# Turning 36 of 96 expert weight pieces in the steps of the first attention stage

## The chip, the cores and the metric

The kernel runs on one core of a Trainium2 chip. The time is device microseconds of one execution, the median of several. Engines are named as the profile names them: PE (TensorE), PEld (its weight loads), DVE (VectorE), ACT (ScalarE), POOL (GpSimd), SP (the queue that starts most DMAs).

## The reference

Two decoder layers on 16 sequences of 64 tokens with 128 features (1024 tokens), each a chain of three blocks, each block followed by the residual sum and a layernorm:

```python
x = ln(x + L0_attn(x))            # 16 heads of 8, rope, causal
x = ln(x + L0_xattn(x, ctx))      # 16 heads of 8, padding mask
x = ln(x + L0_ffn(x))             # 8 experts, inner 512, best 2 of 8 for each token
x = ln(x + L1_attn(x))            # 16 heads of 64
x = ln(x + L1_xattn(x, ctx))
x = ln(x + L1_ffn(x))             # ternary weights, gelu, layernorm inside
```

The third block is what the weights of the change belong to:

```python
for e in range(8):
    hidden = silu(x @ wg[e].T) * (x @ wu[e].T)     # wg, wu: 512 x 128
    out += combine[e] * (hidden @ wd[e].T)         # wd: 128 x 512
```

The matrix unit needs all three of them transposed. One expert has 3 matrices of 4 square pieces of 128x128, so 8 experts have 96 pieces. All is float32.

## The kernel before

The 1024 tokens are 8 tiles of 128. The two first blocks (`a0`, self attention with rope, and `a1`, cross attention; class `Narrow`) are one stream `pre` of 16 tiles. `stream_pe`, `stream_act`, `stream_dve` and `stream_pool` each walk through 18 steps j = 0 to 17. In step j, PE does in this order: the scores of tile j-2 (`s_pe`, L540 to L551), the transpose of the attention output of tile j-5 (`y_pe`, L583), q and k of tile j (`qk_pe`, L512), v of tile j-2 (`v_pe`, L524), the transposes of the probabilities of tile j-3 (`t_pe`, L430), the output projection of tile j-5 (`o_pe`, L587), the weighing of v of tile j-4 (`va_pe`, L567), and the transpose of a finished tile (`x_pe`, L372). ACT does in step j: `y_act` (L633), `qk_act` (L601 or L610), `v_act` (L621), `pt_act` (L439), `exp_act` (L420), `x_act` (L377). DVE does `y_dve` (L677, L681), `max_dve` (L404, L414), `r_dve` (L389, L325, L327), `qk_dve` (L642 to L654, or L667). POOL does the blocks of k (L691), rope's cosine product (L703) and the square root and normalization of the layernorm. Each engine works strictly in its own order, and semaphores join them.

k of a tile lands in columns 0 to 127 of PSUM bank 6 (`B_K`) and q in the same columns of bank 7 (`B_Q`). Columns 128 to 511 of both are unused in these steps.

The expert weights lie in `WALL`, [128, 8 experts, 3 matrices, 512]. SP starts their loads: experts 0 to 3 directly after the masks, experts 4 to 7 after the wide attention's weights. All 24 loads raise one semaphore, `s_raw`.

After the stream comes a written-out part, the drain (`drain_pe`, `drain_act`, `drain_dve`, `drain_pool`), in which the last tiles of `a1` end, the router's logits are made, the two best experts of each token chosen (`choose`), the row of each token in the sorted list found (`place`), and the tokens scattered to DRAM by POOL's indirect DMAs (`scatter`, L1438). Between these steps of PE and ACT stand 24 groups of weights: `weights_pe` turns one matrix (4 pieces) in one of banks 0 to 3, `weights_copy` copies the 512 columns back in place. Groups 0 to 9 are strewn between the drain's steps, 10 to 12 stand before the last `rank_pe`, 13 to 23 behind it.

Then the routed block runs (`moe.pe` and its partners): 23 blocks of 128 sorted rows, each loaded from DRAM (`XG`), turned (L1522), multiplied with the gate (L1550), up (L1558) and down (L1581) weights. Its first instruction on PE waits for the last copy of weights and for the first block's load, which SP starts once all 16 scatters have landed.

Of the kernel before, what the change touches and what calls it, by code (L numbers as in the profile page):

```python
# [15 lines left out]
P = 128  # L16
# [5 lines left out]
PAIRS = HEADS // 2  # L22
EXPERTS, INNER = 8, 512
CH = INNER // P
BANK = 512
LN_EPS = 1e-5

# [51 lines left out]
def decoder_kernel(nc, A, out):  # L79
    with ExitStack() as ctx:  # L80
# [142 lines left out]
        s_b = [sem("first_biases_loaded"), sem("second_biases_loaded")]  # L223
        s_m = sem("masks_loaded")
        s_raw = sem("expert_weights_loaded")
        s_wide = sem("wide_weights_loaded")
        s_out_w = sem("wide_output_weights_loaded")
        s_sep = sem("wide_weights_separated")
# [949 lines left out]
        def stream_pe(pe, tiles, extra, last):  # L1178
            for j in range(last):
                a = at(tiles, j - 2)  # L1180
                if a:
                    a.stage.s_pe(pe, a)
                y = at(tiles, j - 5)
                if y:
                    y.stage.y_pe(pe, y)
                b = at(tiles, j - 1)
                if b:
                    b.stage.qkw_pe(pe, b)
                b = at(tiles, j)
                after_v = a and a.stage.wide  # L1190
                if b and not after_v:
                    b.stage.qk_pe(pe, b)
                if a:
                    a.stage.v_pe(pe, a)
                extra(pe, j, False)
                t, v = at(tiles, j - 3), at(tiles, j - 4)
                if v and v.stage.wide:
                    v.stage.va_pe(pe, v)
                if t:
                    t.stage.t_pe(pe, t)  # L1200
                if v:
                    v.stage.ty_pe(pe, v)
                first_v = v and not v.stage.wide and y and y.stage.wide
                if first_v:
                    v.stage.va_pe(pe, v)
                if y:
                    y.stage.o_pe(pe, y)
                if v and not first_v and not v.stage.wide:
                    v.stage.va_pe(pe, v)
                if v:  # L1210
                    v.stage.vb_pe(pe, v)
                if b and after_v:
                    b.stage.qk_pe(pe, b)
                for x in turned(tiles, j):
                    x.stage.x_pe(pe, x)
                extra(pe, j, True)
# [96 lines left out]
        class Routed:  # L1313
# [3 lines left out]
            def __init__(self, prev):  # L1317
                self.prev = prev
                self.w_mm, self.w_cp = Mark("expert_weights_transposed"), Mark("expert_weights_copied")
                self.g_mm, self.lg = Mark("logits_made"), Mark("logits_copied")  # L1320
                self.top, self.topi, self.topf = Mark("logits_sorted"), Mark("experts_ranked"), Mark("ranked_experts_cast")
                self.oh, self.sel, self.bef = Mark("choices_made"), Mark("choices_joined"), Mark("choices_counted")
                self.r_mm, self.rk, self.pm, self.posf, self.pos = (
                    Mark("ranks_made"), Mark("ranks_based"), Mark("ranks_chosen"), Mark("rows_summed"), Mark("rows_made"))
                self.map = Mark("blocks_mapped")
                self.diff, self.e2, self.den = Mark("logit_difference_made"), Mark("second_exponential_made"), Mark("pair_sum_made")
                self.p1, self.p2 = Mark("first_weight_made"), Mark("second_weight_made")
                self.xt_mm, self.xgt = Mark("block_transposed"), Mark("block_copied")
                self.gate_mm, self.u_mm, self.silu, self.mul = (
                    Mark("gates_projected"), Mark("ups_projected"), Mark("silu_made"), Mark("hidden_made"))  # L1330
                self.d_mm, self.ycp = Mark("downs_projected"), Mark("expert_output_copied")
                self.we_act, self.we_pool = Mark("first_blocks_weights_brought"), Mark("blocks_weights_brought")
                self.acc = Mark("expert_added")
                self.norm = Norm("experts")


            def weights_pe(self, pe, g):
                e, w = g // 3, g % 3
                if g == 0:
                    pe.wait_ge(s_raw, 48 * EXPERTS)  # L1340
                if g >= 4:
                    pe.wait_ge(*self.w_cp.at(g - 3))
                elif g >= 2:
                    pe.wait_ge(*pre[-1].pt_read(g - 2))
                else:
                    pe.wait_ge(*pre[-1].s_read())
                for c in range(CH):
                    m = pe.transpose(PS[:, g % 4, P * c:P * (c + 1)], WALL[:, e, w, P * c:P * (c + 1)], ident)
                m.then_inc(self.w_mm.sem, 1)

            def weights_copy(self, act, g):
                act.wait_ge(*self.w_mm.at(g + 1))
                act.activation(WALL[:, g // 3, g % 3, :], PS[:, g % 4, :], ACT.Copy).then_inc(self.w_cp.sem, 1)


            def logits_pe(self, pe, k):
# [171 lines left out]
                act.activation(XGT[:, j % 3, :], PS[:, 6, 0:P], ACT.Copy).then_inc(self.xgt.sem, 1)  # L1528

            def bring_act(self, act, j, e):  # L1530
                act.wait_ge(*self.w_cp.at(3 * EXPERTS))
                act.activation(WE[:, j % 3].rearrange("p w i -> p (w i)"),
                               WALL[:, e, 0:2, :].rearrange("p w i -> p (w i)"), ACT.Copy).then_inc(self.we_act.sem, 1)

# [57 lines left out]
            def pe(self, pe):  # L1592
                last = pre[-1]
                pe.wait_ge(*last.y_read())
                pe.wait_ge(*self.rk.at(len(GROUPS)))
                pe.wait_ge(*self.map.at(8))
                _, e = nc.values_load_multi_w_load_instructions(
                    bi[0:1, 0, 0:BLOCKS], engines=[mybir.EngineType.PE], min_val=0, max_val=EXPERTS - 1,
                    skip_runtime_bounds_check_because="a sum of seven comparisons, each 0 or 1")
                pe.wait_ge(*self.w_cp.at(3 * EXPERTS))  # L1600
                self.block_pe(pe, 0)
                self.block_pe(pe, 1)
                for n in range(BLOCKS + 1):
                    if n + 2 < BLOCKS:
                        self.block_pe(pe, n + 2)
                    if n == 8:
                        fc.totals(pe, self.mul.at(n - 1))
                    if n < BLOCKS:
                        self.gate_pe(pe, n)
                    if n == 9:  # L1610
                        pe.wait_ge(*fc.thr.at(2))
                    if n < BLOCKS:
                        self.up_pe(pe, n)
                    if n >= 1:
                        self.down_pe(pe, n - 1, e[n - 1])
                pe.wait_ge(s_sep, 3)
                pe.wait_ge(*self.silu.at(BLOCKS))
                wide.weights_pe(pe)
                pe.wait_ge(*self.xgt.at(BLOCKS))
                fct.pe(pe, [0])  # L1620
                pe.wait_ge(*self.ycp.at(BLOCKS))
                fct.pe(pe, [1])
                pe.wait_ge(*self.mul.at(BLOCKS))
                wide.products_pe(pe)
                fc.project_bias(pe)
                fc.means_pe(pe)
                pe.wait_ge(*fc.bias.at(1))
                self.turn_pe(pe, (0,))
# [50 lines left out]
            def pool(self, pool):  # L1679
# [1 line left out]
                _, e = nc.values_load_multi_w_load_instructions(  # L1681
                    bi[0:1, 0, 0:BLOCKS], engines=[mybir.EngineType.Pool], min_val=0, max_val=EXPERTS - 1,
                    skip_runtime_bounds_check_because="a sum of seven comparisons, each 0 or 1")
                pool.wait_ge(*self.w_cp.at(3 * EXPERTS))
                for j in range(2, BLOCKS):
                    self.bring_pool(pool, j, e[j])
                    if j in (6, 9, 12):
# [91 lines left out]
                (moe.rank_pe if late else moe.logits_pe)(pe, 0)  # L1779

        def pre_act(act, j, late):
            if j == 1 and late:
                later.copies(act, 0)
            if j in (2, 3) and late:
                weights.copies(act, 0, [j - 2])
            if j == len(pre) and not late:
                moe.logits_act(act, 0)
# [38 lines left out]
        def drain_pe(pe):  # L1826
# [25 lines left out]
            moe.logits_pe(pe, 3)  # L1852
            weights_pe(pe, 10, 13)
            moe.rank_pe(pe, 3)
            weights_pe(pe, 13, 3 * EXPERTS)

        def drain_act(act):
            moe.logits_act(act, 1)
# [14 lines left out]
            moe.x_act(act, 7)  # L1873
            weights_act(act, 9, 10)
            moe.logits_act(act, 3)
            weights_act(act, 10, 3 * EXPERTS)
            act.activation(warm[:, 0:1], half[:, :], ACT.Silu)

        def drain_dve(dve):
# [64 lines left out]
        def _(sp):  # L1944
# [19 lines left out]
                    load(mri[half + 2 * j:half + 2 * j + 2, :, :], mask[:, 0], s_m)  # L1964

            def load_expert(e):
                for w, name in enumerate(("L0_ffn_wg", "L0_ffn_wu")):
                    load(WALL[:, e, w].rearrange("p (c h) -> p c h", c=CH),
                         A[name][e].rearrange("(c i) h -> i c h", c=CH), s_raw)
                load(WALL[:, e, 2], A["L0_ffn_wd"][e], s_raw)  # L1970

            for e in range(4):
                load_expert(e)
# [102 lines left out]
```

## Time and profile before

| | us |
|---|---|
| median of 3 runs | 368.32 (366.67 to 368.34) |
| the profiled execution, whole | 367.42 |
| its span, first to last instruction | 365.6 |

Times in the profile run from the start of the span. The profiled execution has 1.8 us around its span. PE is busy for 90% of the span. The engines' rows in the timeline end with the idle time ahead of the group, in brackets, and what ended it.

### The profile page before, as it was taken

How to read it: one execution, taken by the hardware profiler on the slowest of the kernel's cores; microseconds unless marked ns; L12 is line 12 of the kernel's file. 1: busy time of each engine (PE TensorE's matmuls, PEld its weight loads, DVE VectorE, ACT ScalarE, POOL GpSimd, SP SyncE). 2: the span in 40 equal slices, each digit the busy share in tenths (PEclk: the TensorE clock that was granted, in tenths of full speed). 3: DMA queues.
4: the chain of work that ended last, by engine and by line, in shares of the span. 5: the costliest groups of instructions: out<-in, count | busy, mean ns of one | idle time of the engine just before them, and what ended most of it. 6: DMA issues, size and time to landing. Idle time of an engine off the chain costs nothing.

```text
span 365.6 us, 9896 instructions
## 1 busy us (share of the span) xinstructions
PE 328.4 (90%) x3774; PEld 259.7 (71%) x3774; DVE 236.4 (65%) x561; ACT 182.6 (50%) x383; POOL 203.0 (56%) x289
## 2 busy tenths in 40 slices
PE   3879999998888599999995997899999999999993
PEld 2546767777677499999994864676677676777673
DVE  2698987778865034573337477845666677877685
ACT  2457766777578533233313243453355436667641
POOL 2856998885777155543306755321222257486785
PEclk9989999999999699999998799999999999999998
DMA  6899997000001111111101110000000000000001
GB/s 184 229 310 285 293 336 203 2 2 3 31 29 53 58 31 52 50 46 45 39 22 38 46 31 14 2 2 2 0 4 2 1 2 3 2 2 2 4 22 38
DMA packets 35993, 22.98 MB, mean 63 GB/s; under 512 B 4196, under 2 KB 33900, under 8 KB 35820
## 3 DMA queue, kind: packets, MB, share of 16 engines
q1 hardware_dynamic: 34636, 19.64, 18.5%
q0 software_dynamic: 1024, 2.10, 1.9%
q8 instruction: 31, 0.51, 0.6%
q10 hardware_dynamic: 288, 0.62, 0.5%
q14 instruction: 14, 0.11, 0.1%
HBM read 14.61 MB, written 7.73 MB: 61 GB/s over the span
## 4 chain that ended last, share of the span: by engine, by line
PE 71%; DVE 15%; issue 5%; POOL 3%; ACT 3%; DMA 2%; SPq 1%; POOLq 0%; ACTq 0%; DVEq 0%
PE banks L845 7%; PE banks L430 7%; PE banks L832 7%; PE banks L1550 6%; PE banks L1558 6%; PE banks L1581 6%; PE banks L540 5%; PE banks L567 5%; PE banks L876 3%; PE banks L512 2%; PE banks L524 2%; PE banks L1033 2%; DVE mx L404 2%; PE banks L583 2%; PE banks L859 2%
## 5 line engine op out<-in xcount | busy, mean ns | idle before, releaser
L691 POOL TENSOR_TENSOR KB<-KT,cst 128x512 f32<-128x512 f32 x48 | 49.3, 1048 | 7.8 <-DVE KT L651 5.6
L404 DVE TENSOR_REDUCE mx<-banks 128x16 f32<-128x1024 f32 x32 | 38.6, 1206 | 12.0 <-PE banks L551 10.1
L439 ACT ACTIVATE PT<-banks 128x512 f32<-128x512 f32 x64 | 34.7, 594 | 23.0 <-PE banks L430 21.8
L882 ACT ACTIVATE U<-banks 128x512 f32<-128x512 f32 x40 | 23.9, 597 | 37.6 <-PE banks L845 22.6
L1573 DVE TENSOR_TENSOR PT<-banks,PR 128x512 f32<-128x512 f32 x23 | 15.9, 691 | 41.1 <-PE banks L1558 36.8
L1538 POOL COPY U<-WALL 128x1024 f32 x21 | 21.9, 1043 | 35.7 <-PE banks L1558 35.5
L332 POOL TENSOR_SCALAR ve<-mv 128x1 f32<-128x1 f32 x40 | 9.2, 231 | 50.8 <-DVE mv L327 50.4
L420 ACT ACTIVATE PR<-PR 128x1024 f32<-128x1024 f32 x32 | 33.9, 1058 | 4.0 <-DVE PR L414 3.7
L430 PE MATMUL banks<-cst,PR 128*128 128x128 f32 x256 | 34.8, 279 | 0.5 <-POOL PR L911 0.5
L832 PE MATMUL banks<-XT,WQKV 128*128 128x128 f32 x256 | 32.8, 290 | 0.4 <-ACT XT L1751 0.4
L845 PE MATMUL banks<-WALL,XT 128*64 128x512 f32 x128 | 29.8, 601 | 3.1 <-DVE U L882 2.8
L832 PEld LDWEIGHTS banks<-XT,WQKV 128*128 128x128 f32 x256 | 31.3, 203 | 1.1 <-ACT XT L1751 0.7
L540 PE MATMUL banks<-KB,QS 64*64 64x512 f32 x192 | 27.9, 635 | 3.6 <-DVE PR L414 2.2
L430 PEld LDWEIGHTS banks<-cst,PR 128*128 128x128 f32 x256 | 27.6, 141 | 4.1 <-issue 2.0
L414 DVE TENSOR_TENSOR PR<-banks,mx 128x1024 f32<-128x1024 f32 x24 | 29.4, 1224 | 0.8
L567 PE MATMUL banks<-VB,PT 128*64 128x18 f32 x768 | 26.7, 212 | 0.0
L567 PEld LDWEIGHTS banks<-VB,PT 128*64 128x64 f32 x768 | 24.3, 138 | 3.0 <-issue 0.5
L1550 PE MATMUL banks<-XGT,U 128*128 128x128 f32 x184 | 25.3, 282 | 0.0
L882 DVE COPY U<-banks 128x512 f32<-128x512 f32 x24 | 16.2, 686 | 13.7 <-PE banks L845 10.9
L334 POOL TENSOR_TENSOR rstd<-ve,half 128x1 f32<-128x1 f32 x40 | 23.2, 579 | 3.3
L1707 POOL DMA_INDIRECT KB<-routed_rows,pos x16 | 15.9, 993 | 16.4 <-DMA routed_rows<-YS 12.3
L1581 PE MATMUL banks<-WALL,PT 128*128 x184 | 24.4, 276 | 0.6 <-DVE YS L1589 0.6
(192 smaller groups left out, 700.0 us busy)
## 6 DMA issues: line engine op xcount, KB each, us to landing
routed_rows<-zero SPq DMA_DIRECT2D x1, 4544.0 KB, 19.3
WALL<-in_L_ffn_wg_dram SPq DMA_DIRECT2D x8, 256.0 KB, 5.0
WALL<-in_L_ffn_wu_dram SPq DMA_DIRECT2D x8, 256.0 KB, 5.3
WALL<-in_L_ffn_wd_dram SPq DMA_DIRECT2D x8, 256.0 KB, 5.6
U<-in_L_attn_W_qkv_dram SPq DMA_DIRECT2D x1, 1536.0 KB, 23.0
XG<-routed_rows SPq DMA_DIRECT2D x23, 64.0 KB, 1.8
routed_rows<-YS SPq DMA_DIRECT2D x23, 64.0 KB, 1.6
cst<-shape_constants ACTq DMA_DIRECT2D x1, 537.0 KB, 4.5
```

The costliest lines, as they stand in the source:

```text
L404: dve.tensor_reduce(mx[:, n % 2, :], s, AX.X, ALU.max).then_inc(self.max.sem, 1)
L420: act.activation(p, p, ACT.Exp, scale=self.scale).then_inc(self.exp.sem, 1)
L430: t = pe.transpose(PS[:, B_PT + m, P * (r % 4):P * (r % 4 + 1)], PR[:, n % 2, P * r:P * (r + 1)], ident)
L439: act.activation(PT[:, n % 2, 4 * m:4 * m + 4, :].rearrange("p r q -> p (r q)"), PS[:, B_PT + m, :], ACT.Copy).then_inc(self.pt.sem, 1)
L540: pe.matmul(PS[q, B_S + g, :], QS[f, n % 3, q], KB[f, n % 2, b].rearrange("p h k -> p (h k)"), start=True, stop=False)
L567: m = pe.matmul(PS[64 * b:64 * b + 64, B_Y, w * r:w * (r + 1)], PT[:, n % 2, r, 64 * b:64 * b + 64], VB[:, n % 3, r, b].rearrange("p a e - ...
L691: pool.tensor_tensor(KB[:, n % 2, b], bc(KT[:, n % 2, b, :], 1, 8), bc(cst[:, C_HEAD:C_HEAD + 8], 2, SEQ), ALU.mult).then_inc(self.kb.sem, 1)
L832: m = pe.matmul(PS[:, bank, P * k:P * (k + 1)], WQKV[:, f // 2, P * u:P * (u + 1)], XT[:, P * i:P * (i + 1)], start=True, stop=True)
L845: m = pe.matmul(PS[64 * a:64 * a + 64, bank, :], XT[:, SEQ * (2 * i + b):SEQ * (2 * i + b + 1)], WVO[:, a, 4 * g:4 * g + 4, :].rearrange(" ...
L882: return eng.activation(o, s, ACT.Copy) if part == 0 else eng.tensor_copy(o, s)
L1550: m = pe.matmul(PS[:, j % 2, P * c:P * (c + 1)], WE[:, j % 3, 0, P * c:P * (c + 1)], XGT[:, j % 3, :], start=True, stop=True)
L1581: m = pe.matmul(PS[:, 7, 0:P], HT[:, j % 2, c, :], WALL[:, e, 2, P * c:P * (c + 1)], start=(c == 0), stop=(c == CH - 1))
```

## The change

The pieces of experts 0, 1 and 2 (36 of 96) are turned in steps 3 to 9 of the stream, 3 pieces at a time. Steps 3 to 7 have two groups each, one in columns 128 to 511 of the k bank and one in those of the q bank; steps 8 and 9 have one each, in the q bank. On PE they stand between `s_pe` and `y_pe`; on ACT each group is copied back by one instruction of 384 columns at the end of the step. PE waits, before it writes a bank again, for the copy of the group that was in it; step 10 waits for all 12. The loads of experts 0, 1 and 2 get a semaphore each. The drain has 15 groups of 4 pieces in place of 24; its written-out order is the same up to group 12, and 2 groups, not 11, stand behind the last `rank_pe`.

```diff
@@ stream_pe
                 if a:
                     a.stage.s_pe(pe, a)
+                if tiles is pre:
+                    moe.early_pe(pe, j)
                 y = at(tiles, j - 5)
@@ class Routed
+            def pieces(self, j):
+                if not 3 <= j <= 9:
+                    return []
+                first, banks = (6 * (j - 3), (B_K, B_Q)) if j <= 7 else (30 + 3 * (j - 8), (B_Q,))
+                return [(first // 3 + k, bank) for k, bank in enumerate(banks)]
+
+            def early_pe(self, pe, j):
+                if j == 10:
+                    pe.wait_ge(*self.e_cp.at(4 * EARLY))
+                for g, bank in self.pieces(j):
+                    if g % 4 == 0:
+                        pe.wait_ge(s_raw0[g // 4], 48)
+                    if bank == B_K or j > 7:
+                        for s in pre[j - 1].stage.qk_read(pre[j - 1].i):
+                            pe.wait_ge(*s)
+                    if g >= 2:
+                        pe.wait_ge(*self.e_cp.at(g - 1 if j <= 7 else g))
+                    w = WALL[:, g // 4].rearrange("p w i -> p (w i)")
+                    for n in range(3):
+                        k = 3 * (g % 4) + n
+                        m = pe.transpose(PS[:, bank, P * (n + 1):P * (n + 2)], w[:, P * k:P * (k + 1)], ident)
+                    m.then_inc(self.e_mm.sem, 1)
+
+            def early_act(self, act, j):
+                for g, bank in self.pieces(j):
+                    act.wait_ge(*self.e_mm.at(g + 1))
+                    w = WALL[:, g // 4].rearrange("p w i -> p (w i)")
+                    k = 3 * (g % 4)
+                    act.activation(w[:, P * k:P * (k + 3)], PS[:, bank, P:4 * P], ACT.Copy).then_inc(self.e_cp.sem, 1)
+
             def weights_pe(self, pe, g):
-                e, w = g // 3, g % 3
+                e, w = EARLY + g // 3, g % 3
                 if g == 0:
-                    pe.wait_ge(s_raw, 48 * EXPERTS)
+                    pe.wait_ge(s_raw, 48 * (EXPERTS - EARLY))
@@ pre_act
+            if late:
+                moe.early_act(act, j)
@@ drain_pe (drain_act likewise)
             moe.rank_pe(pe, 3)
-            weights_pe(pe, 13, 3 * EXPERTS)
+            weights_pe(pe, 13, 3 * (EXPERTS - EARLY))
```

## Rows read from the trace of the kernel before

**Rows 1.** The page, busy time of PE: us, share, instructions.
```profile
PE 328.4 (90%) x3774; PEld 259.7 (71%) x3774; DVE 236.4 (65%) x561; ACT 182.6 (50%) x383; POOL 203.0 (56%) x289
```
**Rows 2.** The chain that ended last, steps 9 and 10: start us, us, what.
```profile
51.14 1.02 PE banks L540 x8
52.38 0.26 PE banks L583
...
56.02 1.02 PE banks L540 x8
```
**Rows 3.** The same chain, steps 4 and 5.
```profile
24.57 1.84 PE banks L540 x8
...
26.83 1.15 PE banks L512 x4
...
28.47 1.02 PE banks L430 x8
...
31.77 0.27 PE banks L583
```
**Rows 4.** Timeline of PE, 20 to 128 us: start, us, work, idle before.
```profile
21.79 0.60 PE L271 MATMUL banks<-cst,U 128*128 128x128 f32 x4
24.57 1.84 PE L540 MATMUL banks<-KB,QS 64*64 64x512 f32 x8 [2.18 <-DVE PR L414]
...
36.95 0.33 PE L583 MATMUL banks<-cst,ysb 128*128 128x128 f32 x1 [0.56 <-DVE ysb L681]
...
42.14 0.33 PE L583 MATMUL banks<-cst,ysb 128*128 128x128 f32 x1 [0.24 <-DVE ysb L681]
...
47.43 0.33 PE L583 MATMUL banks<-cst,ysb 128*128 128x128 f32 x1 [0.34 <-DVE ysb L681]
...
112.78 5.00 PE L1348 MATMUL banks<-cst,WALL 128*128 128x128 f32 x44
```
**Rows 5.** Timeline of ACT, steps 6 and 7, and the drain's end.
```profile
41.02 0.28 ACT L377 ACTIVATE XT<-banks 128x128 f32<-128x128 f32 x1
42.50 0.37 ACT L633 ACTIVATE yT<-banks,bvc 128x128 f32<-128x128 f32 x1 [1.20 <-PE banks L583]
...
113.45 5.50 ACT L1353 ACTIVATE WALL<-banks 128x512 f32<-128x512 f32 x11 [0.84 <-PE banks L1348]
```
**Rows 6.** Timeline of DVE, step 6.
```profile
39.40 0.29 DVE L389 TENSOR_TENSOR R<-banks,XR 128x128 f32<-128x128 f32 x1
...
41.79 0.29 DVE L681 TENSOR_TENSOR ysb<-banks,rs 128x128 f32<-128x128 f32 x1
```
**Rows 7.** Timeline of SP's queue: the last load of expert 0.
```profile
15.95 0.50 SPq L1946 DMA_DIRECT2D WALL<-in_L_ffn_wd_dram  x1
```
**Rows 8.** DMA issues, 15.9 to 16.4 us: count, size, us to landing.
```profile
WALL<-in_L_ffn_wd_dram SPq DMA_DIRECT2D x1, 256.0 KB, 3.9
```
**Rows 9.** Windows of 1 us: five engines' busy, granted clock, DMA.
```profile
27.00:28.00 1.00, 1.00 (x6) 0.78 (x8) 1.00 (x1) 0.37 (x1) 0.82 (x1) 0.50 1.21 316
28.00:29.00 1.00, 1.00 (x13) 0.93 (x14) 0.96 (x2) 0.83 (x3) 0.54 (x1) 0.90 1.09 295
...
117.00:118.00 1.00, 0.79 (x8) 0.55 (x5) 0.00 (x0) 1.00 (x3) 0.70 (x1) 1.00 0.19 66
```
**Rows 10.** The chain that ended last, end of drain and first block.
```profile
118.00 2.23 DMA routed_rows<-X,pos
...
120.40 1.75 DMA XG<-routed_rows
...
122.29 0.46 PE banks L1522
...
124.55 1.72 PE banks L1550 x8
```
**Rows 11.** Timeline of POOL, its last scatter.
```profile
118.00 0.96 POOL L1438 DMA_INDIRECT routed_rows<-X,pos  x1 [0.30 <-issue]
```
**Rows 12.** The copies of weights, line L1353: min, median, max ns, first and last start.
```profile
L1353 ACT ACTIVATE WALL<-banks x24: 591/601/703, 101.2 to 118.2; 128x512 f32<-128x512 f32 x24
```

More of the change, by code:

```diff
@@ L24 @@
 CH = INNER // P
+EARLY = 3
 BANK = 512
@@ L225, in decoder_kernel @@
         s_raw = sem("expert_weights_loaded")
+        s_raw0 = [sem("first_expert_weights_loaded_%d" % e) for e in range(EARLY)]
         s_wide = sem("wide_weights_loaded")
@@ L1319, in __init__ @@
                 self.w_mm, self.w_cp = Mark("expert_weights_transposed"), Mark("expert_weights_copied")
+                self.e_mm, self.e_cp = Mark("early_weights_transposed"), Mark("early_weights_copied")
                 self.g_mm, self.lg = Mark("logits_made"), Mark("logits_copied")
@@ L1352, in weights_copy @@
                 act.wait_ge(*self.w_mm.at(g + 1))
-                act.activation(WALL[:, g // 3, g % 3, :], PS[:, g % 4, :], ACT.Copy).then_inc(self.w_cp.sem, 1)
+                act.activation(WALL[:, EARLY + g // 3, g % 3, :], PS[:, g % 4, :], ACT.Copy).then_inc(self.w_cp.sem, 1)
             def logits_pe(self, pe, k):
@@ L1530, in bring_act @@
             def bring_act(self, act, j, e):
-                act.wait_ge(*self.w_cp.at(3 * EXPERTS))
+                act.wait_ge(*self.w_cp.at(3 * (EXPERTS - EARLY)))
                 act.activation(WE[:, j % 3].rearrange("p w i -> p (w i)"),
@@ L1599, in pe @@
                     skip_runtime_bounds_check_because="a sum of seven comparisons, each 0 or 1")
-                pe.wait_ge(*self.w_cp.at(3 * EXPERTS))
+                pe.wait_ge(*self.w_cp.at(3 * (EXPERTS - EARLY)))
                 self.block_pe(pe, 0)
@@ L1683, in pool @@
                     skip_runtime_bounds_check_because="a sum of seven comparisons, each 0 or 1")
-                pool.wait_ge(*self.w_cp.at(3 * EXPERTS))
+                pool.wait_ge(*self.w_cp.at(3 * (EXPERTS - EARLY)))
                 for j in range(2, BLOCKS):
@@ L1875, in drain_act @@
             moe.logits_act(act, 3)
-            weights_act(act, 10, 3 * EXPERTS)
+            weights_act(act, 10, 3 * (EXPERTS - EARLY))
             act.activation(warm[:, 0:1], half[:, :], ACT.Silu)
@@ L1966, in load_expert @@
             def load_expert(e):
+                s = s_raw0[e] if e < EARLY else s_raw
                 for w, name in enumerate(("L0_ffn_wg", "L0_ffn_wu")):
                     load(WALL[:, e, w].rearrange("p (c h) -> p c h", c=CH),
-                         A[name][e].rearrange("(c i) h -> i c h", c=CH), s_raw)
-                load(WALL[:, e, 2], A["L0_ffn_wd"][e], s_raw)
+                         A[name][e].rearrange("(c i) h -> i c h", c=CH), s)
+                load(WALL[:, e, 2], A["L0_ffn_wd"][e], s)
             for e in range(4):
```

## The prediction

> **What bounds the kernel now.** I read the page first: PE is busy for 90% of the span [rows 1]. That share is an average, so the two stretches that the change touches, the stream's steps 3 to 10 and the drain's end, were read in the chain of waits and in each engine's timeline.
>
> In the steady stream PE is the bound. Step 9's scores start at 51.14 and step 10's at 56.02, a period of 4.88 us, and the chain is made of PE alone; scores to the next transpose of y (`y_pe`) take 1.24 us [rows 2]. Whatever is put on PE there is paid in full. In steps 6 to 8 PE stands still for 0.56, 0.24 and 0.34 us ahead of `y_pe`, each time for DVE's `ysb` [rows 4]; this is just where the early groups go. DVE itself waits there for PE's output projection: from its sum R at 39.40 to the end of `ysb` at 42.08 it takes 2.7 us, and then PE goes on [rows 6]. So these steps are a loop through both engines, and PE's room in it is no more than its idle time. In step 3 there is more: PE has done its last work there by 22.4 and waits 2.18 us for DVE's subtraction before step 4 begins at 24.57 [rows 4].
>
> At the drain's end, the last 11 groups take PE from 112.78 to 117.8 and ACT to 118.95 [rows 4, 5]. The first block does not wait for them. Its transpose starts at 122.29, after the tile's load (120.40, 1.75 us), which itself follows POOL's last scatter (issued 118.00, landed 120.23) [rows 10, 11]. Between the last copy and that transpose lie 3.3 us.
>
> **What goes: nine groups at the end of the drain.** Groups 0 to 12 keep their places, so the drain's own chain stays. Of the 11 groups behind the last `rank_pe` two remain: PE ends some 4 us and ACT 9 x 0.5 = 4.5 us earlier [rows 5]. What is late next is what was late before, the scatters on POOL, which wait for no weights. ACT's work between its last copy and the first block moves forward with the copy and was finished in time anyway. I count the gain as 0.
>
> **What comes: 36 transposes on PE.** 44 of them took 5.0 us at the full clock, so 0.113 apiece, 0.34 for a group of three, 0.67 for a step with two groups [rows 4, 9]. No row has a copy of 384 columns. 128 columns took 0.28 us and 512 took 0.60 [rows 5, 12]; these two are its bounds, and the value on the line between them is 0.49, which I take. The copies of a step are 0.98 us on ACT. Behind them in ACT's queue stands the next step's `y_act`, ahead of which ACT idles 1.20 us [rows 5], waiting for `y_pe`, which now comes later still; so they delay no other work of ACT. What they can delay is PE: the second group of a step waits for the second copy of the step before, and `y_pe`, q, k, v and the probabilities' transposes are queued behind it.
>
> Step by step, as the lateness of `y_pe` (or of the scores) against the trace of before:
>
> Step 3: the early groups come up at 19.8 us. The last load of expert 0 is issued at 15.95 and lands 3.9 us later, at 19.85 [rows 7, 8], just in time. The 0.67 us goes into the 2.18 us of idle time that follows. DVE's work there is queued behind its own subtractions and does not notice. Cost 0; without that cover it would be 0.67.
>
> Step 4: here the granted clock is at its lower level, 1.2 GHz, having fallen in the idle time before: 0.50 until 28 us, 0.90 in the next one [rows 9]. In this stretch the scores take 1.84 us against 1.02 [rows 2, 3]. The six transposes stand at 26.83, 0.67 x 2 = 1.34 us at half clock. They use up the slow time, so q, k and v after them run at the full clock: about 0.83 us in place of the 1.64 between 26.83 and 28.47 [rows 3]. Net +0.53.
>
> Step 5: +0.67, and about 0.10 of waiting: ACT's exponential follows PE's transposes, and its two copies end 0.4 us after the scores, while PE's first group fills only 0.34. `y_pe`, at 31.77 before [rows 3], comes 1.30 late.
>
> Step 6: two groups, but 0.56 us of idle time [rows 4] take most of it, since the loop through DVE brings `ysb` at its own pace. +0.25, total 1.55.
>
> Step 7: idle time 0.24, and with the small gap before it 0.31. ACT's `x_act` ended at 41.30 [rows 5], 4.35 us after `y_pe` at 36.95; two copies and a semaphore make 5.4, and one group 0.34 more: `y_pe` 5.74 us after the last one, where it was 5.19 [rows 4]. +0.55, total 2.10.
>
> Step 8: one group, which waits for both copies of step 7: +0.13, total 2.23. Step 9: one group in a step bound by PE, less a rest of idle time: +0.27, total 2.50. Step 10 waits for one copy that is 0.3 us early. From there every step is bound by PE and the lateness is carried to the end.
>
> Sum: 2.5 us on the profiled execution's 367.42 us (365.6 of span, 1.8 around it): 369.9. That execution lies 0.9 under the median of the three runs; the middle of all four executions is 367.9. I add the 2.5 to that: 370.4.
>
> Bounds: at the lower end the copies never hold PE (-0.4) and the clock does not fall before step 4 (-1.0, below): +1.1. At the upper end none of steps 4 to 9 has room: 30 transposes x 0.113 = 3.4, with the copy waits (0.5) and a whole extra 0.67 at half clock: +4.6.
>
> A rule of the Trainium skill speaks against the change more strongly. During 44 transposes in a row the granted clock stayed at 1.00 and each took 0.113 us [rows 4, 9]. The page "TensorE: Matmul & The Clock Gate", Part 4 (PE-mode transpose), says that the full clock is not engaged by transposes. By that rule the early groups would run at 0.225 us apiece, 36 x 0.113 = 4 us more than here, and the sum would be up to 6.5. The trace doesn't agree with it, and I give it no share.
>
> **The rivals.**
>
> A, the clock stays up in step 4. With the early groups in step 3, PE's idle time ahead of 24.57 shrinks from 2.18 to about 1.5 us. For it: less idle time than the gap that the clock fell in. Against it: 1.5 us is still a gap, and the work before it is the same. If so, the scores of step 4 take 1.24 instead of 2.26 with their masks, and `y_pe` of step 5 comes about 1.0 earlier: +1.5, 368.9 on the profiled execution, 369.4 on the middle. Half of that would be within what can be told.
>
> B, ACT becomes the loop. Copies of 0.60 rather than 0.49 and a longer way from copy to PE (0.15 more) add 2 x 0.11 + 0.15 = 0.37 to each of the steps 5 to 8, 1.5 us in all: +4.0, 371.9. For it: ACT's last copy of step 6 ends, by my sum, at almost the moment at which PE's first group does. Against it: 512 columns took 0.60, and 384 should take less.
>
> C, faster: the last copies do hold the first block. If the first block's transpose followed the last copy and not the load, the end of the drain would come up to 4.5 us earlier, and with the 2.5 paid in the stream the time would be 2.0 less: 365.9. It decides only if ACT's last copy, or what follows it, ends after the tile's load. For it: the block's first instruction does wait for that copy. Against it: 3.3 us lie between them, and POOL's last scatter is issued 0.95 us before the last copy ends, and lands 1.3 after [rows 5, 10, 11].
>
> D, the weights come too late. If expert 0 lands some 4 us after the early groups come up, q and k of tile 3 and the first transposes of probabilities wait behind them, 2.2 us of which the idle time doesn't take: +4.7, 372.6. For it: at 19.85 against 19.8 there is no margin. Against it: up to 1.5 us of lateness is covered.
>
> **How the numbers follow.** Forecast 0.50 (369.0 to 371.6), A 0.23, B 0.11, C 0.09, D 0.07. Predicted 370.4. The range 368.5 to 372.4 takes in the forecast, A's middle, B and the lower half of D, and leaves out C and the tails. What a measurement of this kernel can tell from no change is about 0.5%, 1.8 us. Forecast is over that in eight cases of ten (0.40), A in a third (0.08), B and D always (0.18): 0.66, of which I take off 0.06 for the chance in the runs: slower 0.60. C and a little of A: faster 0.09. The rest, 0.31, is the same.
>
> **What would show it.** Period of the scores in steps 5 to 8: about 5.6, 5.5 and 5.4 us in place of 5.2, and 4.88 again from step 10. The first block's transpose at about 124.8, as far behind POOL's last scatter as before, with PE idle ahead of it for some 8 us in place of 4.5. ACT's early copies at 0.49. The granted clock near 25 us separates A. A period above 6 us in step 6 or 7, with PE waiting for ACT, would be B; a first block's transpose at under 122 us would be C; PE idle near 20 us for the load, D. I am wrong if the scores of step 12 stand less than 1 us later than before, or if the stretch from the last scatter to the first block has shrunk.

## The result: 0.4% slower, and the clock decides over as much as the change

| | before | after |
|---|---|---|
| median us (20 runs each) | 367.65 (366.28 to 371.79) | 368.72 (367.56 to 370.24) |
| profiled execution, whole / span | 367.42 / 365.6 | 370.17 / 368.4 |

The ratio is 1.0041 with a 95% interval of 1.0028 to 1.0055: 1.5 us (1.0 to 2.0); the two medians lie 1.1 apart. The forecast was +2.5 us (370.4); its range of 368.5 to 372.4 holds the measured 368.7 at its lower edge, and the size is the +1.5 of rival A. Part of that agreement is luck, as the comparison of single profiles below shows.

The profile after. Here is the page's line of busy time; beside [rows 1], the work on PE is the same.

```profile
PE 328.7 (89%) x3774; PEld 260.7 (71%) x3774; DVE 236.3 (64%) x561; ACT 182.9 (50%) x386; POOL 202.8 (55%) x289
```

The timeline of PE after, steps 3 to 9, where [rows 4] had its idle times (scores L542, early groups L1363, `y_pe` L585):

```profile
20.77 0.87 PE L1363 MATMUL banks<-cst,WALL 128*128 128x128 f32 x6 [0.63 <-DMA WALL<-in_L_ffn_wd_dram]
...
24.79 1.09 PE L542 MATMUL banks<-KB,QS 64*64 64x512 f32 x8 [0.86 <-issue]
25.67 0.43 PE L550 MATMUL banks<-caus,idb 64*64 64x512 bf16 x4
26.30 0.84 PE L1363 MATMUL banks<-cst,WALL 128*128 128x128 f32 x6 [0.21 <-ACT WALL L1371]
...
29.97 1.09 PE L542 MATMUL banks<-KB,QS 64*64 64x512 f32 x8
...
31.92 0.27 PE L585 MATMUL banks<-cst,ysb 128*128 128x128 f32 x1
...
37.19 0.27 PE L585 MATMUL banks<-cst,ysb 128*128 128x128 f32 x1
...
42.72 0.27 PE L585 MATMUL banks<-cst,ysb 128*128 128x128 f32 x1
...
47.96 0.27 PE L585 MATMUL banks<-cst,ysb 128*128 128x128 f32 x1
...
56.73 1.09 PE L542 MATMUL banks<-KB,QS 64*64 64x512 f32 x8
```

The idle times ahead of `y_pe` are gone, so is most of that ahead of step 4, and step 4's scores take 1.09 us where they took 1.84: the clock did not fall there. PE is now the bound from step 5 on: `y_pe` comes every 5.27, 5.53 and 5.24 us. In windows around step 4, before, then after (the number behind the five engines is the granted clock):

```profile
24.00:28.00 4.00, 3.44 (x18) 1.53 (x20) 3.57 (x8) 1.42 (x2) 3.13 (x4) 0.60 1.14 317
```
```profile
24.00:28.00 4.00, 3.00 (x31) 1.92 (x32) 3.90 (x9) 2.61 (x6) 3.31 (x5) 1.00 1.13 316
```

By step 10 the scores stand at 56.73 against 55.95, only 0.78 us later, and 0.23 of that was there at step 3. At step 12 it is 0.79 (66.48 against 65.69). The profiled execution is 2.8 us longer in all, and lost most of the rest, 1.8 us, at two places where nothing was added. One is the drain's start (1.2 us up to the first block), where the clock fell at 92.8, after PE's 1.07 us of idle time at 90.7, an idle time that the kernel before has too. Windows of 1 us, after; then PE's timeline there, whose row before took 1.09 us for the same transposes:

```profile
92.00:93.00 1.00, 1.00 (x12) 0.34 (x12) 0.90 (x6) 0.28 (x1) 0.66 (x2) 0.91 0.00 0
93.00:94.00 1.00, 1.00 (x9) 0.18 (x1) 0.67 (x3) 0.00 (x0) 0.89 (x2) 0.50 0.00 0
```
```profile
91.73 0.30 PE L374 MATMUL banks<-cst,X 128*128 128x128 f32 x1 [1.07 <-issue]
...
94.65 1.84 PE L432 MATMUL banks<-cst,PR 128*128 128x128 f32 x8
```

The other is the first block, which begins at 124.28, 4.42 us behind POOL's last scatter where it was 4.29 [rows 10, 11]: the relief brought nothing. PE had been idle for 8.56 us, not 4.51, and the clock rose 6.1 us after the first transpose, not 4.9. From that transpose to the first product with `wd` (called the cold start below) it took 7.67 us (before: 7.10).

```profile
124.28 0.45 PE L1558 MATMUL banks<-cst,XG 128*128 128x128 f32 x1 [8.56 <-DMA XG<-routed_rows]
...
126.34 1.93 PE L1586 MATMUL banks<-XGT,U 128*128 128x128 f32 x8
128.06 1.92 PE L1594 MATMUL banks<-XGT,U 128*128 128x128 f32 x8
...
131.95 1.06 PE L1617 MATMUL banks<-WALL,PT 128*128 x8
```

So one profile of each does not give the price of the change: it has other falls of the clock in it. The executions of all comparisons but the 20 of the kernel before in the table have their mean granted clock on record, and the spans come in lots by it. Of 111 executions of the kernel before, 42 have a mean of 0.977 or 0.978 and a median span of 364.6 us, 57 have 0.973 and 366.1, and 12 lie between 366.7 and 371.1. Of 34 after, 19 have 0.973 and 366.4, 13 have 0.969 or 0.964 and 368.1, and two have 370.2 and 371.1. Lot against lot the change costs 1.8 and 2.0 us, if the lots are paired from the best down. More executions are in the better lot after (19 of 34 against 42 of 111), which gives part of it back. (After, the mean is lower at equal losses, since the clock is down for longer around PE's idle time ahead of the first block: 10.2 us in the profile with doubled copies below, whose mean is 0.973, against 6.8 in the second profile before, at 0.978.) The mean tells how long the clock was down and not where, so that this pairing is argued, not shown.

### The profile page after: what moved, and what is told of

It is laid out like the page before. It is cut to its first block, busy times and chain, and to the rows that moved or that the text cites. A ratio compares the mean times of both kernels' runs of the same rounds, so it can differ in the third digit from the quotient of the medians.

```text
span 368.4 us, 9909 instructions
## 1 busy us (share of the span) xinstructions
PE 328.7 (89%) x3774; PEld 260.7 (71%) x3774; DVE 236.3 (64%) x561; ACT 182.9 (50%) x386; POOL 202.8 (55%) x289
## 4 chain that ended last, share of the span: by engine, by line
PE 75%; DVE 11%; issue 5%; POOL 3%; ACT 2%; DMA 2%; SPq 1%; POOLq 0%; DVEq 0%; ACTq 0%
PE banks L432 8%; PE banks L847 7%; PE banks L834 7%; PE banks L569 6%; PE banks L1586 6%; PE banks L542 6%; PE banks L1594 6%; PE banks L1617 6%; PE banks L878 3%; PE banks L514 2%; PE banks L526 2%; PE banks L1035 2%; PE banks L861 2%; PE banks L374 1%; PE banks L1091 1%
## 5 line engine op out<-in xcount | busy, mean ns | idle before, releaser
L1609 DVE TENSOR_TENSOR PT<-banks,PR 128x512 f32<-128x512 f32 x23 | 15.9, 691 | 41.8 <-PE banks L1594 37.5
L432 PE MATMUL banks<-cst,PR 128*128 128x128 f32 x256 | 35.6, 283 | 0.5 <-POOL PR L913 0.5
L542 PE MATMUL banks<-KB,QS 64*64 64x512 f32 x192 | 27.2, 617 | 2.5 <-issue 2.5
L1586 PE MATMUL banks<-XGT,U 128*128 128x128 f32 x184 | 25.4, 283 | 0.0
L1594 PE MATMUL banks<-XGT,U 128*128 128x128 f32 x184 | 25.2, 281 | 0.0
```

Of the source, the lines that this page charges most:

```text
L432: t = pe.transpose(PS[:, B_PT + m, P * (r % 4):P * (r % 4 + 1)], PR[:, n % 2, P * r:P * (r + 1)], ident)
L542: pe.matmul(PS[q, B_S + g, :], QS[f, n % 3, q], KB[f, n % 2, b].rearrange("p h k -> p (h k)"), start=True, stop=False)
L1586: m = pe.matmul(PS[:, j % 2, P * c:P * (c + 1)], WE[:, j % 3, 0, P * c:P * (c + 1)], XGT[:, j % 3, :], start=True, stop=True)
L1594: m = pe.matmul(PS[:, 2 + j % 2, P * c:P * (c + 1)], WE[:, j % 3, 1, P * c:P * (c + 1)], XGT[:, j % 3, :], start=True, stop=True)
```

## The experiments

All are compared with the kernel before on the same chip. "Shift" is the start of the scores of a step, counted from those of step 3 of the same profile; before it is 37.35 us for step 10, after 37.90.

**The kernel before and after once more.** No edit.

> The kernel before once more, for a second profile. Theory: two lots, near 364.6 us of span at a mean clock of 0.977 and near 365.8 at 0.973; a profile of the first shows no fall ahead of step 4 and scores of step 10 some 0.9 us earlier than 55.95. If the lots come from anything else than the clock, the scores stand where they stood.

Median 367.71, ratio 1.0006 (0.9984 to 1.0028). This profile is one of the better lot (0.978, span 365.0). PE's idle time of 2.18 us ahead of step 4 is the same, yet the clock stayed up:

```profile
24.67 1.09 PE L540 MATMUL banks<-KB,QS 64*64 64x512 f32 x8 [2.18 <-DVE PR L414]
...
29.26 1.09 PE L540 MATMUL banks<-KB,QS 64*64 64x512 f32 x8 [0.19 <-DVE PR L414]
```

Step 5's scores come 4.59 us after step 4's, where the first profile had 5.90, and step 10 stands at a shift of 36.37, 0.98 less. The same kernel with the same idle time does the one or the other. The 3.4 us at half clock in step 4 also make up the 0.005 between the two profiles' means (0.973 and 0.978). The 0.98 us are two thirds of the 1.5 between the lots, and for the other 0.5 there is no row.

> The changed kernel once more, for a second profile. Theory (price of the moved groups 1.5 us against a kernel before whose clock stays up in step 4, and the rest is the clock): step 4 at the upper level again, and executions in two lots, near 366.1 us of span without a fall of the clock in the drain and near 368.1 with one. If the fall at 93 us of the first profile belongs to the change, it is in nearly all executions.

Median 368.95, ratio 1.0041 (1.0023 to 1.0060), as at first. The theory held for the lots (8 of 14 near 366.5, 4 near 368.2) but not for this profile, which shows a third thing, span 371.1:

```profile
21.80 1.54 PE L1363 MATMUL banks<-cst,WALL 128*128 128x128 f32 x6 [1.51 <-DMA WALL<-in_L_ffn_wd_dram]
23.14 1.06 PE L514 MATMUL banks<-XT,WT 128*128 128x128 f32 x4
24.13 0.70 PE L526 MATMUL banks<-WT,XT 128*64 128x64 f32 x8
24.75 1.97 PE L432 MATMUL banks<-cst,PR 128*128 128x128 f32 x8
26.52 1.06 PE L273 MATMUL banks<-cst,U 128*128 128x128 f32 x4
27.51 1.09 PE L542 MATMUL banks<-KB,QS 64*64 64x512 f32 x8
```

SP issued expert 0's last load 0.54 us later than in the first profile before, and it took 5.3 us to land instead of 3.9. PE waited 1.51 us from 20.3 on, the clock fell at 20.7, and the rest of step 3 ran at half of it: step 4's scores begin at 27.51, 8.52 us after step 3's, where all other profiles have 5.96 or 5.97: 2.6 us late. So rival D is real, by another way than it was priced: a wait of 1.5 us was to be covered, and what was not covered is the work at half clock. Of 34 executions after, two have spans over 370, this one among them. The clock also fell once in this profile's drain, at 106.0.

**The stream alone.** The early copies go to a spare tile; the drain keeps its 24 groups.

```diff
-   act.activation(w[:, P * k:P * (k + 3)], PS[:, bank, P:4 * P], ACT.Copy)
+   act.activation(SCRATCH[:, g % 6, :], PS[:, bank, P:4 * P], ACT.Copy)
```

> The 12 early groups as in the changed kernel, but copied to a spare tile, and the drain with all its 24 groups: the price of the stream alone. My theory (the drain's relief is worth nothing, the whole difference is PE time in the stream): the same as the changed kernel, 1.0 to 1.9 us above before, near 368.8. Rival (the relief gives back part of a larger price): clearly slower than the changed kernel, 2.5 us or more above before.

Median 369.14, ratio 1.0057 (1.0033 to 1.0081): the change's price without its relief. The shift of step 10 is 37.91, as after, and the last scatter to first block takes 4.37 us. The two ratios lie 0.6 us apart and both are uncertain, so a relief of up to 1.6 us isn't excluded by them; 2.5 us or more is. The lots say less: 366.7 (7 executions at 0.977 and 0.978) and 368.2 (4 at 0.973 and 0.974), 2.1 us over the kernel before in both, where the change had 1.8 and 2.0.

**The relief alone.** `weights_pe(pe, 13, 15)` and its copies in place of groups 13 to 23, nothing early.

> Before, with the last nine groups of the drain left out and nothing added (those weights stay unturned, so that the result is another; the routing is decided ahead of them and stays): the relief alone. My theory: within 0.4 us of before, and the first block's transpose stands as far behind POOL's last scatter as before, with PE idle for 8 us. Rival (the last copies hold the first block): 2 to 4.5 us faster. A second rival (the longer idle time costs clock): 0.5 to 1.5 us slower, with the granted clock at its lower level for longer after the first block.

Median 368.11, ratio 1.0047 (1.0011 to 1.0083). No gain, and by the ratio not the 0 that I expected either. The first block is 4.41 us behind the last scatter, with PE idle for 8.56. The clock went down at 117.9 instead of 120.4 and rose at 128.1 instead of 127.2, and the first block took 7.50 us to its first product instead of 7.10. The ratio lies elsewhere: nine of its 12 executions correspond to the kernel before's lot of 366.1 (they have 365.8), three to the one near 370, and none to that of 364.6. So within a lot the relief changed 0.3 us or less. Why the best lot is missing stays open: it turns on step 4, which this kernel has unchanged and where its profile lost the clock. On this chip 9 of 35 executions before are in that lot, so that 12 in a row outside it would come by chance some three times in a hundred. It was not run again.

**Step 3 alone.** The two early groups of step 3, to the spare tile, whole drain.

> Before, with the two early groups of step 3 alone (copied to a spare tile, the drain whole). Theory of the clock (they shorten PE's idle time ahead of step 4, the clock stays at its upper level there): 0.4 to 0.9 us faster than before, with step 4 at the full clock in the profile. Rival (only the work counts, and it hides in the idle time): the same within 0.2, and the clock falls as in before. If even this cover fails: 0.7 slower.

Median 368.09, ratio 0.9986 (0.9944 to 1.0029): the time does not tell. The profile does: step 4 runs at the upper clock, with 0.82 us of idle time ahead of it:

```profile
24.62 1.09 PE L543 MATMUL banks<-KB,QS 64*64 64x512 f32 x8 [0.82 <-issue]
```

The shift of step 10 is 36.43 against 37.35 and, with the clock up, 36.37. The six transposes cost 0.06 us. This profile, too, has the clock down at the drain's start, from 90.5 to 93.9. It lies in the lot at 0.973 without a fall in step 4. The best lot (5 of 12, at 0.978) has 365.2, which is 0.6 over the kernel before's, not 0.06.

**No group in step 3.** Two groups in each of steps 4 to 7, one in each of 8 to 11. Of the edit this is the main line; the groups are numbered to match, and step 12 waits for all of them.

```diff
-                if not 3 <= j <= 9:
+                if not 4 <= j <= 11:
```

> The changed kernel with its 12 groups in steps 4 to 11 (two a step to 7, then one), none in step 3. Theory: the cover of step 3 is gone, so 6 more transposes are paid (0.7 us), and the clock falls ahead of step 4 again in most executions (0.5 to 0.9): 1.2 to 1.6 us above the changed kernel, 370.0 to 370.4. Rival (what counts is only the number of transposes on PE, wherever they stand): the same as the changed kernel.

Median 371.94, ratio 1.0132 (1.0094 to 1.0170): 4.9 us over before, 3.4 over the change, more than expected. Step 4's scores again have 2.18 us of idle time ahead of them, the clock is at 0.50 from 26 to 29 us, and the six transposes there took 1.54 us:

```profile
24.75 1.09 PE L542 MATMUL banks<-KB,QS 64*64 64x512 f32 x8 [2.18 <-DVE PR L416]
25.98 1.54 PE L1363 MATMUL banks<-cst,WALL 128*128 128x128 f32 x6
...
31.18 1.09 PE L542 MATMUL banks<-KB,QS 64*64 64x512 f32 x8
```

At step 12 the shift is 1.91 us more than after and 2.47 more than before. Both sides have the clock down in step 4 in the second comparison, and in the first only this kernel has. All five executions on record lie at mean clocks of 0.964 to 0.969; the profiled one also lost the clock at the drain's start, which makes up about 1 us of the rest.

**Groups in steps where PE is the bound.** One group of three in each of steps 9 to 15, spare tile, whole drain.

> Before, with seven groups of three transposes in steps 9 to 15, one a step, in the q bank (copied to a spare tile, the drain whole). In these steps PE is the bound and nothing idles. Theory (a group costs its 0.34 to 0.36 us in such a step, and its copy on ACT nothing): 2.4 to 2.5 us above before in executions with the same granted clock, steps of 5.23 us in place of 4.87. Rival (PE reads weights for the next work early and swallows part of it): under 1.5 us.

Median 369.99 of seven executions, ratio 1.0085 (1.0054 to 1.0116), 3.1 us. The lot at 0.978 (four of them) has 367.65 against 364.6, +3.0. The profile is of the slowest execution, with the clock down in step 4 and from 103.7 on besides, but at 1.00 in steps 9 to 16. There the steps are 5.20 us long:

```profile
51.12 1.09 PE L543 MATMUL banks<-KB,QS 64*64 64x512 f32 x8
52.35 0.55 PE L1361 MATMUL banks<-cst,WALL 128*128 128x128 f32 x3
52.74 0.27 PE L586 MATMUL banks<-cst,ysb 128*128 128x128 f32 x1
...
56.32 1.09 PE L543 MATMUL banks<-KB,QS 64*64 64x512 f32 x8
```

A group costs 0.33 us, seven 2.3, and nothing of it is swallowed. The other 0.7 is not in the stream; I have no row for it. The stream alone and step 3 alone have such a surplus too, as said in the next section.

**The copies twice.**

```diff
+                    act.activation(SCRATCH[:, g % 6, :], PS[:, bank, P:4 * P], ACT.Copy)
                     act.activation(w[:, P * k:P * (k + 3)], PS[:, bank, P:4 * P], ACT.Copy)
```

> The changed kernel with every early copy of ACT done twice (first to a spare tile): some 0.8 us more on ACT in each of steps 3 to 7, 0.4 in 8 and 9. The prediction said that the copies already hold PE by 0.1 to 0.2 us a step; by that, each step from 5 to 8 would grow by most of 0.8 and the time by 2.5 to 3 us over the changed kernel. What the profile after says (the second copy ends some 0.3 us before PE's second group asks for it): 0.3 to 0.5 a step, 1.5 to 2 us in all. If ACT has room: nothing.

Median 371.96 of six executions, ratio 1.0159 (1.0106 to 1.0212), 3.2 us over the change's median, and 3.5 in the lot at 0.973 (369.9 against 366.4); the shift of step 10 is 3.20 more (41.10). PE now waits for ACT's copies in each of steps 4 to 8, for example in step 8:

```profile
48.97 1.09 PE L543 MATMUL banks<-KB,QS 64*64 64x512 f32 x8
...
51.04 0.52 PE L1364 MATMUL banks<-cst,WALL 128*128 128x128 f32 x3 [0.77 <-ACT WALL L1375]
```

Steps 4 to 8 are 0.4 to 0.8 us longer, for 0.74 us more of copies (0.37 each). So the copies of the change stand 0 to 0.3 us short of holding PE: ACT's margin is small, yet my copy waits were not there.

**Fills on the changed kernel.** Transposes of the identity into a free bank, read by nobody, 64 of them between the drain and the first block.

```diff
             drain_pe(pe)
+            for _ in range(64):
+                pe.transpose(PS[:, B_Y, 0:P], ident, ident)
```

> The changed kernel with 64 transposes of the identity put on PE in its idle time ahead of the first block (7.2 us of some 8.5), which nobody reads. If the cold start of the first block costs what its rows show (gate, up and gate again 1.7, 1.7 and 1.0 us against 0.9 each), it ends 1.3 to 1.9 us under the changed kernel, near 367.0, and no slower than before. If the first block is bound by its waits and not by the clock: 368.7, and if the filling stands in the way: more.

Median 369.53, ratio 1.0039 (1.0000 to 1.0077): no gain. The clock was still up as the first block began at 123.44, but between the lone transposes of blocks 0 to 2 PE idles 0.46 us twice, after 1.96 us of idle time that the fill had left. The clock fell at 124.5, and gate and up took 1.93 and 1.53 us.

**Fills on the kernel before, in the gaps too.** 12 at the end of step 3, 8 in step 16, 38 behind the drain, and 3 behind each of the first two block transposes.

```diff
                 self.block_pe(pe, 0)
+                filler(pe, 3, B_Y)
                 self.block_pe(pe, 1)
+                filler(pe, 3, B_Y)
```

> Before, with nothing moved, but transposes of the identity that nobody reads in PE's idle times: 12 at the end of step 3, 8 in step 16 ahead of the last transposes of x, 38 behind the drain and 3 each between the first blocks. Theory of the clock (what the changed kernel won in step 4 and lost in the drain is the clock alone): step 4, the drain and the first block run at the upper level, 0.9 and 1.3 to 1.6 us off, 365.0 to 365.8 in the median, and the fills delay nothing. Rival (the fills stand in the way or the clock falls all the same): 367.6 or more.

Median 365.77 (363.99 to 368.20), ratio 0.9972 (0.9945 to 1.0000). Of all kernels here it has the lowest median; the gain over the kernel before is at the edge of the interval, that over the changed one is clear of it. The clock does fall once, in the drain at 101.3. Step 4, the drain's start and the first block are at the upper clock, and the fills delay nothing:

```profile
118.08 4.31 PE L1180 MATMUL banks<-cst 128*128 128x128 f32 x38
122.86 0.30 PE L1532 MATMUL banks<-cst,XG 128*128 128x128 f32 x1 [0.47 <-DMA XG<-routed_rows]
...
124.53 1.11 PE L1560 MATMUL banks<-XGT,U 128*128 128x128 f32 x8
125.47 1.06 PE L1568 MATMUL banks<-XGT,U 128*128 128x128 f32 x8
```

From the first transpose to the first product with `wd` it takes 5.40 us, here and in the two filled kernels that follow, against 6.89 to 8.03 in the profiles without fills at this place: the cold start had cost 1.7 before.

**The same fills on the changed kernel** (8, 72 and twice 3; step 3 has its own groups).

> The changed kernel with unread transposes of the identity in PE's idle times: 8 in step 16, 72 behind the drain, 3 each between the first blocks. Theory: the drain and the first block at the upper level; what is left against the kernel before with the same kind of fills (363.6 to 363.9 us of span at most clocks) is the price of the stream, 1.5 us: about 365.3 of span, 367 in the median, 1 to 2 us under the changed kernel. Rival (the moved groups cost nothing once the clock is taken care of): the same as the filled kernel before.

Median 366.99, ratio 0.9987 (0.9965 to 1.0009). Executions with the highest mean (0.995) have 364.4 here (five) and 362.35 in the filled kernel before (two), those at 0.986 to 0.988 have 365.0 (four) and 363.8 (six): the price of the moved groups is 1.2 to 2.1 us. The profile is one of the two slowest (0.978) and had the clock down in the drain, from 102.5 to 108.6; the shift of step 10 in it is 37.91, against 36.38 in the filled kernel before.

**Two more fills in the drain** (7 ahead of the second `y_pe`, 6 ahead of the last ranks).

> The filled kernel before, with two more fills: 7 unread transposes ahead of the drain's second transpose of y (PE idled 0.91 us there in the filled kernel's profile, and the clock fell 1.2 us later) and 6 ahead of the last ranks (0.78 us idle). Theory: the fall of the clock at 101 us goes, at most 1.2 us of span, so 362.4 rather than 363.6 in most executions and a median near 365.0. Rival (that fall does not come from this idle time, or the fills hold up the ranks' chain): the same as the filled kernel or up to 1 us more.

Median 366.74, ratio 0.9987 (0.9962 to 1.0011). The rival was right about the time: only 2 of 12 executions have means above 0.990, and the median is no better. The profile has no fall of the clock in the drain any more, and POOL issues its last scatter at a shift of 98.38 instead of 99.49. But that scatter took longer to land (2.23 us in the filled kernel before), and the first block starts at 103.95 against 103.91:

```profile
117.23 3.47 DMA routed_rows<-X,pos
```

So in this profile the 1.1 us that the clock gave back ended in a wait for a DMA. That is one profile; what the landing takes in the others stays open.

## Why the forecast was right in kind and large in size

*By the prediction's own sign it was wrong in the stream.* It said "I am wrong if the scores of step 12 stand less than 1 us later than before". They stand 0.79 us later in the profile after than in the first one before (0.56 as a shift), which is also under the sum's lower bound of 1.1. Against the second profile before, with the clock up, it is 1.53 as a shift. It also gave 0.60 to a slowdown of more than 1.8 us, and the measured one is 1.5 (1.0 to 2.0): slower, but under that line.

*The drain's relief is worth nothing: right, within what the runs can tell.* The first block starts 4.3 to 4.4 us behind POOL's last scatter with 24 groups or 15. Two profiles with fills have 4.80 and 5.57, because the scatter took 2.73 and 3.47 us to land instead of 2.23. The relief alone was no faster. That the longer idle time lengthens the cold start is not shown: the five profiles with some 8.5 us of idle time have 6.98 to 8.03 us (7.5 in the mean), the five with some 4.5 have 6.89 to 7.84 (7.3).

*Transposes cost their time where PE is the bound: right.* A group costs 0.33 us in steps 9 to 15. In the profile after, steps 5 to 7 with two groups each have 0.67 more than PE's bare work.

*The copies hold PE in steps 5 to 8: wrong.* The mis-sized term is the copy. Alone it takes 0.50 us, as I drew it from [rows 5, 12]; but two in a row start 0.37 us apart, so the pair ends 0.88 after its start and not 0.98. The same was to be read from the trace of before: 11 copies of 0.60 in 5.50 us [rows 5]. Besides, I had ACT's `x_act` ending in step 6 where a wait of ACT (0.37 us) had put it, and that wait was gone. Step 4 alone shows a wait for a copy, 0.21 us. From `y_pe` of step 5 to that of step 9 I summed 21.8 us; it is 21.2.

```profile
L1371 ACT ACTIVATE WALL<-banks x12: 473/502/512, 25.7 to 57.0; 128x384 f32<-128x384 f32 x12
```

*The clock falls ahead of step 4: the step of my sum that failed.* I summed a lateness of 1.30 us by `y_pe` of step 5; counted from step 3's scores it is 0.0 (13.09 against 13.10). I took the row of one profile for the kernel's behaviour and gave the other case 0.23. (The window from 24 to 25 us of the first profile before has a mean clock of 0.89, which puts the fall at 24.8, just behind the start of step 4's scores and not ahead of it.) The groups in step 3 cut PE's idle time from 2.18 to between 0.60 and 1.21 us, and the clock stayed up there in the profiles of after, of the stream alone, of step 3 alone, of both fills on the changed kernel and of the doubled copies. In the five profiles without groups or fills in step 3 it fell in four. So rival A was right about the clock. It said +1.5 against the profiled execution, though, and the shift of step 10 grew by 0.55 us against that one and by 1.53 against the one with the clock up. That the ratio over all executions is 1.5 us as well is luck in part.

*Then the stream's price is 1.5 us with the clock up, and the lots say +1.8 to +2.0.* The other 0.3 to 0.5 is not explained. It isn't the cold start after a longer idle time: the stream alone has 4.55 us of idle time as before and a cold start of 6.89, and its lots still are at +2.1, 0.6 over its shift of 1.54. Step 3 alone has 0.6 in its best lot for 0.06 in the stream, and the groups in steps 9 to 15 have 3.0 for 2.3. All of these kernels also load the experts with other semaphores; no run has that change without groups. How often the clock falls at the drain's start before and after stays open too: it did in one of the two profiles after and in neither of the two before, and these are too few.

*Expert 0 is in time: no, but the idle time mostly covered it.* PE waited 0.63 us for it in the first profile after, 0.28 to 0.89 in others, all hidden in the idle time, and 1.51 in the second, which cost 2.6 us. I gave this 0.07.

The page "TensorE: Matmul & The Clock Gate" of the Trainium skill (HAM oscillation) says that idle gaps between bursts of matmuls bring the slow clock back and cost the burst behind them. The trace agrees: behind 4.51 us of idle time the first block's gate and up took 3.1 us, and with fills in the gap they took 1.8. The same page of the Trainium skill says in Part 4 (PE-mode transpose) that the full clock does not engage for transposes. The trace does not agree: in the filled kernel before, 44 transposes of weights and 38 of the identity behind them ran at a granted clock of 1.00, which held until the first block began. No run shows the clock rise under transposes alone.

## What to carry to other kernels

Ask of work that is moved off one stretch whether that stretch was waiting for it, and of the place it goes to what PE's idle time there is, step by step; a group of transposes is nearly free in idle time (0.06 us for two) and costs all of itself (0.33) where PE is the bound. Idle time of PE isn't all the same: work put into a gap ahead of a burst can pay through the clock; that taking work out of a gap costs is not shown here. Where a program's executions fall into lots by mean clock, compare lot with lot, bear in mind that the mean does not tell where the clock was down, and take no single profile for the kernel.

## What the runs showed of the hardware

The same kernel, with the same 2.18 us of idle time on PE at the same place, lost the clock in one profile and kept it in another, 1.0 us apart by step 10. The idle time of 1.07 us at the drain's start was followed by a fall in one of two profiles after and in neither of two before. ACT's copies of 384 columns took 0.50 us each and started 0.37 apart. Transposes of the identity that nobody reads, 38 ahead of the first block and 3 between its first transposes, brought it from 7.10 to 5.40 us up to its first product with `wd`; 64 that stopped 1.96 us early did not keep the clock up. One 256 KB load took 3.9, 4.1, 4.8 and 5.3 us from issue to landing in four executions, and a wait with no margin on it cost 2.6 us in the last of them.
